# A Swin block on one core: one 128-column bias product for both images of a window, row maxima carried in the stacked q

## What is computed

```python
y = _ln(x, norm1_g, norm1_b)
y = jnp.roll(y, (-SS, -SS), axis=(1, 2))
yw = y.reshape(B, nWh, WS, nWw, WS, C).transpose(0, 1, 3, 2, 4, 5).reshape(B * nW, N, C)
qkv = yw @ qkv_w.T + qkv_b
...
attn = jnp.einsum('bhqd,bhkd->bhqk', q * scale, k)
bias = rel_pos_table[jnp.asarray(_REL_IDX.reshape(-1))].reshape(N, N, HEADS)
attn = attn + bias.transpose(2, 0, 1)[None]
attn = attn.reshape(B, nW, HEADS, N, N) + jnp.asarray(_MASK)[None, :, None]
attn = jax.nn.softmax(attn.reshape(B * nW, HEADS, N, N), axis=-1)
o = jnp.einsum('bhqk,bhkd->bhqd', attn, v)
...
o = o @ proj_w.T + proj_b
...
x = shortcut + o
h = _ln(x, norm2_g, norm2_b)
h = jax.nn.gelu(h @ fc1_w.T + fc1_b, approximate=False)
h = h @ fc2_w.T + fc2_b
return x + h
```

## Time and profile before

| | |
|---|---|
| median of three runs | 4173.44 us (4171.96 to 4176.52) |
| profiled execution, its own time | 4173.6 us |
| its span, first to last instruction | 4171.8 us |
| mean granted TensorE clock | 0.994 of full speed |
| busy: TensorE, VectorE, ScalarE, GpSimd | 3995.3, 2933.7, 2726.8, 2122.9 us |
| TensorE weight loads (beside the products) | 3128.2 us |
| bias products L748 | 4096, 332 ns mean |
| q times k products L753 | 8192, 249 ns mean |
| low halves of q and k on VectorE, L615 | 512, 619 ns mean |

### The profile page before, as it was taken

How to read it: one execution, slowest core, us unless ns; L and a number is a source line. 1 busy time by engine, 2 the same in 40 slices (tenths; PEclk the granted TensorE clock), 3 DMA queues, 4 the chain that set the end, 5 groups by cost and what they waited for, 6 DMA issues and landing times.

```text
span 4171.8 us, 170732 instructions
## 1 busy us (share of the span) xinstructions
PE 3995.3 (96%) x72080; PEld 3128.2 (75%) x72080; DVE 2933.7 (70%) x7196; ACT 2726.8 (65%) x5120; POOL 2122.9 (51%) x3476
## 2 busy tenths in 40 slices
PE   3899999999999999999999999999999999999998
PEld 2677777777777777777777777777777777777777
DVE  6677777777767777776777777777677767777774
ACT  1566666666666666666666666666666666666665
POOL 4455555555555555555555555555555455555553
PEclk8999999999999999999999999999999999999999
DMA  2333333333333333333333333333333333333332
GB/s 74 103 107 109 106 110 107 110 107 107 111 103 109 110 107 108 107 111 106 109 107 107 108 109 110 108 106 112 102 110 107 111 103 108 108 108 108 110 111 59
DMA packets 625966, 441.61 MB, mean 106 GB/s; under 512 B 158468, under 2 KB 624756, under 8 KB 625204
## 3 DMA queue, kind: packets, MB, share of 16 engines
q1 hardware_dynamic: 624739, 428.88, 34.8%
q0 software_dynamic: 464, 1.81, 0.1%
HBM read 106.14 MB, written 51.46 MB: 38 GB/s over the span
## 4 chain that ended last, share of the span: by engine, by line
PE 54%; ACT 16%; DVE 10%; issue 9%; DMA 7%; SPq 2%; ACTq 0%; POOL 0%; DVEq 0%; POOLq 0%
PE ps L766 13%; PE ps L718 10%; PE ps L796 9%; DMA sums<-pv_sb 7%; PE ps L753 7%; PE ps L748 6%; PE ps L780 6%; ACT hid L425 5%; ACT v_own L482 5%; DVE k_lo L615 3%; DVE yT_lo L600 3%; ACT probs L408 3%; ACT k_hi L466 2%; SPq L248 2%; DVE q_lo L615 2%
## 5 line engine op out<-in xcount | busy, mean ns | idle before, releaser
L570 DVE TENSOR_REDUCE neg_max<-ps 113x16 f32<-113x784 f32 x1024 | 993.1, 970 | 394.7 <-PE ps L718 386.1
L408 ACT ACTIVATE probs<-ps 113x784 f32<-113x784 f32 x1024 | 831.4, 824 | 492.8 <-PE ps L753 489.5
L796 PE MATMUL ps<-w,hid 128*112 128x128 f32 x7168 | 858.3, 274 | 0.0
L796 PEld LDWEIGHTS ps<-w,hid 128*112 128x112 f32 x7168 | 815.2, 177 | 21.9 <-issue 0.2
L753 PE MATMUL ps<-st_q,st_k 128*49 128x196 f16 x8192 | 700.9, 249 | 0.0
L748 PE MATMUL ps<-bias,eye_k 108*64 108x392 f16 x4096 | 689.8, 332 | 0.6 <-DMA bias<-neg_maxT 0.6
L425 ACT ACTIVATE hid<-ps,col 128x448 f32<-128x448 f32 (+1 forms) x1024 | 511.9, 576 | 231.1 <-PE ps L780 231.1
L766 PE MATMUL ps<-probs,v_own 113*32 113x49 f32 x32768 | 576.5, 210 | 45.0 <-ACT probs L408 34.3
L766 PEld LDWEIGHTS ps<-probs,v_own 113*32 113x32 f32 x32768 | 432.0, 109 | 227.7 <-issue 132.3
L378 POOL TENSOR_TENSOR x_b<-x,fc_b 112x896 f32<-112x896 f32 x128 | 267.7, 2091 | 604.4 <-DVE y_out L563 604.4
L718 PE MATMUL ps<-mx_k,mx_q 128*49 128x196 f16 x8192 | 548.7, 254 | 17.8 <-DMA mx_k<-k_hi 8.8
(11 more groups left out here) (108 smaller groups left out, 6962.8 us busy)
## 6 DMA issues: line engine op xcount, KB each, us to landing
st_k<-k_hi SPq DMA_DIRECT2D x256, 196.0 KB
st_q<-q_hi SPq DMA_DIRECT2D x1024, 49.0 KB
oT_raw<-pv_sb SPq DMA_DIRECT2D x256, 196.0 KB, 2.7
x_in<-in_x SPq DMA_DIRECT2D x224, 196.0 KB
x_res<-in_x SPq DMA_DIRECT2D x224, 196.0 KB
out_y<-y_out SPq DMA_DIRECT2D x224, 196.0 KB
mx_q<-q_hi SPq DMA_DIRECT2D x128, 196.0 KB
mx_k<-k_hi SPq DMA_DIRECT2D x512, 49.0 KB
```

The lines of the kernel that those rows point to most:

```text
L408: nc.scalar.activation(probs[0:KP, w % 2, :].rearrange("p (b c) -> p b c", b=2), ps[0:KP, b:b + 2, 0:HB * WT], ACT.Exp).then_inc(s_exp, 1)
L570: nc.vector.tensor_reduce(neg_max[0:KP, :, w, :], ps[0:KP, 0:2, 0:HB * WT].rearrange("p b (h k) -> p b h k", k=WT), AX_X, ALU.max, negate= ...
L796: last = mm(tokens_of(6)[0:TP, i, :], hid[:, c, i * TP:(i + 1) * TP], w_2[:, c, :], start=(c == 0), stop=(c == CH - 1))
```

## The change

One product per window and bank now writes the bias of both images: its weights are both images' columns of `eye_k` together, 106 rows and 128 columns, and it writes all 128 partitions of the bank. That asks for weights and a moving operand that do not depend on the image, so the maxima leave `bias`: they go into the free fourth row (MAX_ROW = 3) of the first four rows of each block of 32 partitions of `st_q`, where `st_k` now holds 1. `bias` is kept once rather than for each window. The four DMAs of the maxima write `st_q` instead of `bias`, each with 32 pieces of 98 elements where there were 64 of 49.

For that the layouts change. q and k are laid out window by window (w, image, query) where they were image by image, `st_q` has the block of 32 ahead of the group of heads, `neg_max` is ordered to match, and in `max_logits` the second group of a bank begins at column 256, where it began at 196. The set-up fills `st_k` with 1 and not 0, and clears two banks of `ps`. The number of the q times k products, of the maxima products, of the exponentials and of the DMAs stays as it was, and so do all waits.

```diff
@@ -93,7 +93,7 @@
-        bias = sb("bias", [C, 2, NW, HB * WT], F16)
+        bias = sb("bias", [C, 2, HB * WT], F16)
@@ -107,14 +107,14 @@
-        q_hi, q_lo, k_hi, k_lo = (sb(n, [C, 2, BT], F16) for n in ("q_hi", "q_lo", "k_hi", "k_lo"))
+        q_hi, q_lo, k_hi, k_lo = (sb(n, [C, NW, 2, WT], F16) for n in ("q_hi", "q_lo", "k_hi", "k_lo"))
...
-        st_q = [sb(f"st_q{e}", [C, GQ, EQ, 2 * BT], F16) for e in range(2)]
+        st_q = [sb(f"st_q{e}", [C, EQ, GQ, 2 * BT], F16) for e in range(2)]
...
-        neg_max = sb("neg_max", [C, 2, NW, HB])
+        neg_max = sb("neg_max", [C, EQ, NG, NW])
@@ -259,11 +259,10 @@
-                    for par in range(2):
-                        for im in range(2):
-                            row = MAX_ROWS + im
-                            sp.dma_start(bias[row:row + 1, par, :, :].rearrange("p w c -> p (w c)"),
-                                         neg_maxT[HP * par:HP * (par + 1), im, :]).then_inc(s_neg_dma, 16)
+                    for e in range(EQ):
+                        row = 32 * e + MAX_ROW
+                        sp.dma_start(st_q[odd(0)][row:row + 1, e, :, :].rearrange("p g c -> p (g c)"),
+                                     neg_maxT[32 * e:32 * (e + 1), :, :]).then_inc(s_neg_dma, 16)
@@ -463,7 +462,7 @@
-                        nc.scalar.activation(hi[:, j % 2, :], ps[:, bank, 0:BT], ACT.Identity,
+                        nc.scalar.activation(hi[:, :, j % 2, :], ps[:, bank, 0:BT].rearrange("p (w q) -> p w q", w=NW), ACT.Identity,
                                              bias=col[:, b:b + 1]).then_inc(s_hi, 1)
@@ -568,8 +567,9 @@
                 nc.vector.tensor_reduce(
-                    neg_max[0:KP, :, w, :],
-                    ps[0:KP, 0:2, 0:HB * WT].rearrange("p b (h k) -> p b h k", k=WT),
+                    neg_max[0:KP, :, :, w].rearrange("p e g -> p g e"),
+                    ps[0:KP, 0:2, :].rearrange("p b (g c) -> p (b g) c", g=2)[:, :, 0:EQ * WT].rearrange(
+                        "p g (e k) -> p g e k", k=WT),
                     AX_X, ALU.max, negate=True).then_inc(s_max, 1)
@@ -612,8 +612,9 @@
-                        nc.vector.scalar_tensor_tensor(lo[:, j % 2, :], ps[:, bank, 0:BT], col[:, b:b + 1],
-                                                       hi[:, j % 2, :], ALU.add, ALU.subtract).then_inc(s_lo, 1)
+                        nc.vector.scalar_tensor_tensor(lo[:, :, j % 2, :], ps[:, bank, 0:BT].rearrange("p (w q) -> p w q", w=NW),
+                                                       col[:, b:b + 1], hi[:, :, j % 2, :],
+                                                       ALU.add, ALU.subtract).then_inc(s_lo, 1)
@@ -714,8 +715,8 @@
-                        span = slice(im * BT + w * WT, im * BT + (w + 1) * WT)
-                        last = mm(group(im, 0, g), mx_q[edge(n)][:, g, span], mx_k[:, g, :, span],
+                        span = slice((2 * w + im) * WT, (2 * w + im + 1) * WT)
+                        last = mm(group(im, 0, g, 256), mx_q[edge(n)][:, g, span], mx_k[:, g, :, span],
                                   start=True, stop=True)
@@ -744,13 +745,12 @@
                 for b in range(2):
-                    for im in range(2):
-                        mm(ps[HP * im:HP * (im + 1), bank + b, 0:HB * WT], eye_k[0:BIAS_ROWS, kind, im, :],
-                           bias[0:BIAS_ROWS, b, w, :], start=True, stop=False)
+                    mm(ps[:, bank + b, 0:HB * WT], eye_k[0:BIAS_ROWS, kind, :, :].rearrange("p m q -> p (m q)"),
+                       bias[0:BIAS_ROWS, b, :], start=True, stop=False)
```

More of the change, by code:

```diff
@@ L52 @@
 HP = 64
-MAX_ROWS = 2 * WT
-MASK_ROWS = MAX_ROWS + 2
+MAX_ROW = 3
+MASK_ROWS = 2 * WT
 BIAS_ROWS = MASK_ROWS + 8
@@ L285, in body @@
                     sp.dma_start(mx_q[edge(n)][0:C:4, :, :],
-                                 q_hi[:, :, :].rearrange("c m q -> c (m q)")).then_inc(s_mx_dma, 16)
+                                 q_hi[:, :, :, :].rearrange("c w m q -> c (w m q)")).then_inc(s_mx_dma, 16)
                     for e in range(EQ):
                         sp.dma_start(mx_k[32 * e:32 * (e + 1):4, :, e, :],
-                                     k_hi[32 * e:32 * (e + 1), :, :].rearrange("c m q -> c (m q)")
+                                     k_hi[32 * e:32 * (e + 1), :, :, :].rearrange("c w m q -> c (w m q)")
                                      ).then_inc(s_mx_dma, 16)
@@ L298, in body @@
                         sp.dma_start(st_k[odd(1)][term:C:4, :, :],
-                                     kk[:, :, :].rearrange("c m q -> c (m q)")).then_inc(s_st_dma, 16)
+                                     kk[:, :, :, :].rearrange("c w m q -> c (w m q)")).then_inc(s_st_dma, 16)
                         for e in range(EQ):
-                            sp.dma_start(st_q[odd(1)][32 * e + term:32 * (e + 1):4, :, e, :],
-                                         qq[32 * e:32 * (e + 1), :, :].rearrange("c m q -> c (m q)")
+                            sp.dma_start(st_q[odd(1)][32 * e + term:32 * (e + 1):4, e, :, :],
+                                         qq[32 * e:32 * (e + 1), :, :, :].rearrange("c w m q -> c (w m q)")
                                          ).then_inc(s_st_dma, 16)
@@ L330, in _ @@
                 nc.gpsimd.memset(yT_lo[e][:, :, :, :], 0.0)
-                last = nc.gpsimd.memset(st_k[e][:, :, :], 0.0)
+                last = nc.gpsimd.memset(st_k[e][:, :, :], 1.0)
             last.then_inc(s_initp, 1)
@@ L522, in _ @@
             nc.vector.memset(bv_wide, 0.0)
+            nc.vector.memset(ps[:, 0:2, :], 0.0)
             then(nc.vector.memset(v_own[:, :, :, :], 0.0))
@@ L548, in _ @@
             then(nc.vector.scalar_tensor_tensor(part_hi, part_hi, is_part[:, 0:1], part_lo, ALU.mult, ALU.add))
-            nc.vector.tensor_copy(bias[:, :, :, :], part_hi.rearrange("p (b c) -> p b c", b=2).unsqueeze(2).to_broadcast(
-                [C, 2, NW, HB * WT]))
+            nc.vector.tensor_copy(bias[:, :, :].rearrange("p b c -> p (b c)"), part_hi)
             then(nc.vector.tensor_copy(mx_k[:, :, :, :].rearrange("p g e (u k) -> p (g e) u k", k=WT),
@@ L700, in _, with group @@
             pe.wait_ge(s_init, 2)
-            def group(im, bank, g):
-                return ps[HP * im:HP * im + WT, bank + g // 2, (g % 2) * EQ * WT:(g % 2 + 1) * EQ * WT].rearrange(
-                    "p (e q) -> p e q", e=EQ)
+            def group(im, bank, g, step):
+                first = (g % 2) * step
+                return ps[HP * im:HP * im + WT, bank + g // 2, first:first + EQ * WT].rearrange("p (e q) -> p e q", e=EQ)
             def max_logits(n, w, edge):
@@ L725, in max_transposed @@
                     pe.wait_ge(s_pv_sb, NW * n)
-                nc.tensor.transpose(maxT_ps[:, 0:KP], neg_max[0:KP, :, :, :].rearrange("p b w h -> p (b w h)"),
+                nc.tensor.transpose(maxT_ps[:, 0:KP], neg_max[0:KP, :, :, :].rearrange("p e g w -> p (e g w)"),
                                     idn[0:KP, 0:KP]).then_inc(s_maxT, 1)
@@ L746, in logits @@
                 for b in range(2):
-                    for im in range(2):
-                        mm(ps[HP * im:HP * (im + 1), bank + b, 0:HB * WT], eye_k[0:BIAS_ROWS, kind, im, :],
-                           bias[0:BIAS_ROWS, b, w, :], start=True, stop=False)
+                    mm(ps[:, bank + b, 0:HB * WT], eye_k[0:BIAS_ROWS, kind, :, :].rearrange("p m q -> p (m q)"),
+                       bias[0:BIAS_ROWS, b, :], start=True, stop=False)
                     for g in (2 * b, 2 * b + 1):
                         for im in range(2):
-                            span = slice(im * BT + w * WT, im * BT + (w + 1) * WT)
-                            last = mm(group(im, bank, g), st_k[par][:, g, span], st_q[par][:, g, :, span],
+                            span = slice((2 * w + im) * WT, (2 * w + im + 1) * WT)
+                            last = mm(group(im, bank, g, EQ * WT), st_k[par][:, g, span], st_q[par][:, :, g, span],
                                       start=False, stop=(g % 2 == 1))
@@ L907 @@
     place = lambda i, j: (8 * (i // 3) + j) * 4 + 1 + i % 3
-    mxq_fixed = np.zeros((2, C, GQ, 2, NW, WT), np.float16)
+    mxq_fixed = np.zeros((2, C, GQ, NW, 2, WT), np.float16)
     mxq_fixed[:, place(i, j)] = np.eye(WT, dtype=np.float16)[None, :, None, None, None, :]
@@ L911 @@
     eye[0:2 * WT, :, :, 0:WT] = np.tile(np.eye(WT, dtype=np.float16), (2, 1))[:, None, None, :]
-    for im in range(2):
-        eye[MAX_ROWS + im, :, im, 0:WT] = 1
     for kind, c in enumerate(of_kind):
@@ L916 @@
         for r in range(c.start, c.stop):
-            mxq_fixed[kind // 2, place(WS, r), :, :, w, :] = classes[r]
+            mxq_fixed[kind // 2, place(WS, r), :, w, :, :] = classes[r]
             eye[MASK_ROWS + r, kind, :, 0:WT] = apart[r]
```

## The result

The changed kernel takes 4502.28 us (median of 4 runs, 4500.98 to 4504.53). The kernel before took 4173.58 us beside it. The ratio is 1.0783, with a 95% interval of 1.0769 to 1.0796. The forecast was 4533 us with a range of 4460 to 4620.

The account below looks back on a forecast made before the run. TensorE was taken to bound the kernel, its steady windows in series with the step: 6 x 0.44 = 2.64 us plus 0.165 for the first two windows, 2.805 us x 128 steps = 359 us on 4173.6, so 4533 us (4460 to 4620).

Follow-up runs that it names:

- the one with 1.84: The changed kernel with the wide bias products of both banks issued first and then all eight products of q times k: 4308.07 us, a ratio of 1.0312.

## What to carry to other kernels

Before merging two narrow products into a wide one, look at the distance from the pair's start to the next group: if it is that of one product, they already run side by side in separate columns, and there is nothing to save. Then look at what stands beside the new product: going from at most 64 weight columns to 128 and back cost 0.2 us here whatever the product did, so wide and narrow products belong in groups of their own. With the same products and half the changes the kernel took 4308 us and not 4502. And find out how far behind the next loop stands (here VectorE's, 0.03 us) before paying for work taken off the first.

## What I had not expected

- A product with a single moving column costs as much as going into the wide kind and back when it is 128 columns wide between narrower ones: 0.23 us a window, 152 us in all. Its twin of 64 columns costs 13 us.
- TensorE's stops within the products with v look like a late supply of instructions. In the kernel before, 27 distances between starts within these groups are over 0.2 us. In 26 of them the products went on 1.25 to 1.65 us after a transfer of 16 KB on the queue of kind "instruction" (q8) had ended, while the median distance from one such end to the next is 4.8 us; the one left is the stop at the end of the program. The stops go with the speed of the windows and not with the number of instructions: 35 stops and 12.9 us before, 45 and 23.7 us in the kernel with the merge undone, 26 and 8.9 us without any bias, the fewest instructions of all, but 1 and 0.7 us in each kernel whose steady windows take 2.06 us and in the one with 1.84. That the transfers are the cause was not tried.
- The four DMAs of the maxima land in 2.4 us at the median where they took 4.4, with 32 pieces of 196 bytes each instead of 64 of 98. Nobody waits for them.
